# Edge products of a graph layer split into two column halves of TensorE's array

## The reference

```python
xn  = layernorm(x)
agg = segment_sum(edge_weight[:, None] * xn[src], dst, 12500)       # the edge products
h   = relu(((1 + eps) * xn + agg) @ W1.T + b1)
gnn = h @ W2.T + b2
mix = mixer(xn)       # 1x1 product to 768 channels, batch norm, relu, a grouped product, gated linear
                      # attention within groups of 32 channels, a product back to 256 channels, norms
x   = x + gnn + mix
x   = x + ffn(layernorm(x))    # 256 -> 1024 -> 256 with gelu, kept for the top half of the nodes by a routing weight
```

## Time and profile before

| | us |
|---|---|
| median of two runs | 2584.67 |
| the two runs | 2580.34 and 2589.0 |
| span of the profiled execution | 2600.5 |

### The profile page before, as it was taken

One profiled execution on the slowest core, in us unless ns is written; L12 is line 12 of the kernel. 1 busy time (PEld: TensorE's weight loads), 2 busy tenths in 40 slices (PEclk: granted clock), 3 DMA queues, 4 the chain that ended last, 5 costly groups with the idle time before them and its releaser, 6 DMA issues.

```text
span 2600.5 us, 42005 instructions
## 1 busy us (share of the span) xinstructions
PE 2467.0 (95%) x12655; PEld 2165.7 (83%) x12655; DVE 1799.8 (69%) x5988; ACT 1441.2 (55%) x3219; POOL 1793.2 (69%) x1881
## 2 busy tenths in 40 slices
PE   4789999999999999999999999999999999999996
PEld 4777888878888887888888888888788888888886
DVE  8847775776766767667677676676866767767657
ACT  3545665645656656556565565565655656556531
POOL 1247777777777777777777777777777777777600
PEclk9889999999999999999999999999999999999998
DMA  6734444344344343443444434434344344343338
GB/s 205 254 109 117 117 117 124 113 119 124 113 120 121 115 129 113 120 123 114 124 119 118 124 113 120 123 114 129 113 120 124 113 124 119 113 128 113 111 117 282
DMA packets 192004, 333.43 MB, mean 128 GB/s; under 512 B 46286, under 2 KB 133964, under 8 KB 191672
## 3 DMA queue, kind: packets, MB, share of 16 engines
q0 software_dynamic: 86752, 238.17, 31.9%
q1 hardware_dynamic: 105018, 92.42, 11.2%
HBM read 291.99 MB, written 38.46 MB: 127 GB/s over the span
## 4 chain that ended last, share of the span: by engine, by line
PE 79%; DVE 9%; DMA 6%; ACT 4%; issue 1%; POOL 1%; SPq 0%; DVEq 0%
PE bank L1169 24%; PE qkv L1264 13%; PE bank L1276 12%; PE bank L1183 9%; PE bank L1213 6%; PE qkv L1193 4%; DMA work<-in_x 4%; PE qkv L1192 2%; PE bank L1229 2%; PE bank L1238 2%; PE bank L1203 2%; DVE rings L972 1%; DMA xn_dram<-work 1%; DMA rings<-xn_dram,window 1%; POOL rings L778 1%
## 5 line engine op out<-in xcount | busy, mean ns | idle before, releaser
L778 POOL DMA_INDIRECT rings<-xn_dram,window x1764 | 1767.5, 1002 | 592.0 <-issue 381.7
L1169 PE MATMUL bank<-rings 128*128 128x256 f32 x3528 | 891.6, 381 | 28.8 <-DVE rings L972 15.1
L1169 PEld LDWEIGHTS bank<-rings 128*128 128x128 f32 x3528 | 654.9, 190 | 130.0 <-DVE rings L972 30.6
L972 DVE TENSOR_SCALAR rings<-iota,window_dst,window 128x128 f32<-128x128 f32 x1764 | 556.3, 359 | 143.6 <-PE bank L1169 128.6
L1264 PE MATMUL qkv<-work,ffn_weights 128*128 128x256 f32 x1568 | 362.9, 380 | 0.0
L1276 PE MATMUL bank<-ffn_weights,work 128*128 128x256 f32 x1568 | 362.0, 379 | 0.0
L868 ACT ACTIVATE work<-qkv,fb 128x256 f32<-128x256 f32 x392 | 160.0, 473 | 310.1 <-PE qkv L1264 309.6
L1276 PEld LDWEIGHTS bank<-ffn_weights,work 128*128 128x128 f32 x1568 | 297.2, 190 | 40.0
L1264 PEld LDWEIGHTS qkv<-work,ffn_weights 128*128 128x128 f32 x1568 | 293.9, 190 | 37.8
L1183 PE MATMUL bank<-resident,weights 128*128 128x256 f32 x1176 | 280.6, 382 | 0.0
L1183 PEld LDWEIGHTS bank<-resident,weights 128*128 128x128 f32 x1176 | 225.5, 192 | 31.2
(11 more groups left out here) (241 smaller groups left out, 3288.0 us busy)
## 6 DMA issues: line engine op xcount, KB each, us to landing
rings<-xn_dram,window POOLq DMA_INDIRECT x1764, 2.8
xn_dram<-work SPq DMA_DIRECT2D x14, 896.0 KB, 8.4
work<-xn_dram SPq DMA_DIRECT2D x49, 256.0 KB
work<-in_x SPq DMA_DIRECT2D x48, 256.0 KB
out<-work SPq DMA_DIRECT2D x48, 256.0 KB
work<-in_x SPq DMA_DIRECT2D x7, 896.0 KB, 7.8
rings<-in_x SPq DMA_DIRECT2D x6, 896.0 KB, 9.5
rings<-out SPq DMA_DIRECT2D x6, 896.0 KB, 8.5
```

Of the source, the lines that this page charges most:

```text
L778: nc.gpsimd.indirect_dma_start(out=msg[q][:, :], out_offset=None, in_=xn_dram[:, :], in_offset=bass.IndirectOffsetOnAxis(ap=window[t % WIN ...
L972: v.tensor_scalar(sel[k % SEL_RING], iota[:, :], window_dst[b][:, k % SLOTS:k % SLOTS + 1], window[b][:, k % SLOTS, 2:3].bitcast(F32), ALU ...
L1169: te.matmul(agg[h][:, 0:D], sel[k % SEL_RING], msg[q], start=first, stop=last, skip_group_check=True).then_inc(slot_used, 1)
```

## The change

Each edge product becomes two. The first takes columns 0 to 63 of `sel` as its stationary operand and writes partitions 0 to 63 of `agg[h]`; the second takes columns 64 to 127 and writes partitions 64 to 127. Both stream the whole `msg[q]` of 128 x 256. The built program gives the first the array's columns 0 to 63 (tile size 128 x 64, position 0, 0) and the second columns 64 to 127 (position 0, 64); every other matmul of the main part keeps 128 x 128. The semaphore is raised by the second product alone.

```diff
                 pe.wait_ge(sel_ready, i * STEP_SLOTS + (k + 1))
                 pe.wait_ge(msg_landed[q], i * (16 * TURNS) + 16 * (k // RING + 1))
-                te.matmul(agg[h][:, 0:D], sel[k % SEL_RING], msg[q], start=first, stop=last,
-                          skip_group_check=True).then_inc(slot_used, 1)
+                for half in range(2):
+                    r = slice(half * P // 2, (half + 1) * P // 2)
+                    ins = te.matmul(agg[h][r, 0:D], sel[k % SEL_RING][:, r], msg[q], start=first, stop=last,
+                                    skip_group_check=True)
+                ins.then_inc(slot_used, 1)
```

## The result

The changed kernel takes 2779.73 us in the median of two runs (2779.47 and 2779.99), against 2584.67 before: a ratio of 1.0761 (95% interval 1.0739 to 1.0782), 195 us slower. The forecast was 2870 us. The direction held. Of the terms of the sum, those for the order of the passes and for alternating halves were far too large and the one for the borders far too small, and the errors nearly made up for each other.

A forecast was written before the change was run, and what follows sets the result against it. The prediction took PE to bound the kernel; 151 + 85 + 63 - 14 = +285 us on the profiled span of 2600.5 gave 2886, or 2870 us on the median of 2584.67, with an 8 in 10 range of 2700 to 3400.

The forecast's parts named there:

- the order of the passes: At each group's end, the second half runs one pass late: 0.216 us for each of 701 groups, 151 us.
- alternating halves: When PE goes between halves, a matmul starts 0.03 us later for its weights: 85 us (0 to 170).
- the borders: Changes between full and half width, 1402 of them, cost 0.09 us per group: 63 us (0 to 313).
- PE bounds, and the halves run beside each other: In the edge products, what PE does longer the kernel does longer; both column halves run at once, 0.432 us per product.
- serial rival: The two halves of an edge product never run at once: 0.864 us per edge, 3381 us in all; chance 0.22.
- rival of the paired passes: PE runs both halves' first passes together within a group: +70 us, 2655 us in all; chance 0.06.
- the added bounds: Sum of all terms' bounds: +122 to +447 us, 2707 to 3032 us, with 126 us at most for changes of width.
- the nearest row: A late weight load in the old trace, taken as the cost per width change: 0.03 us half, 0.06 full.
- the rival of the emptying: PE empties at each change between full and half width: 313 us in place of 63, 3120 us in all; chance 0.25.
- Waiting: Of PE's own 28.8 us of waiting before edge products, a slower PE loses some: -14 us (0 to -29).

## Why the prediction was right, and where it was wrong

*PE bounds, and the halves run beside each other.* Right: 0.432 us per slot within a group, and the runs with one half alone (no gain) and with both in the same half (688 us more) show it from both sides. The serial rival, 3381 us, is out.

*The order of the passes costs a half edge per group, 151 us.* Wrong, the step that failed. It took the passes to start in the order of the program, so that the second half runs one pass late. They start in pairs, 6 to 7 ns apart, and the run with the halves apart shows that another product between the two halves in the kernel doesn't hinder it: the pairs are 13 to 14 ns apart there. The term measured nothing. The rival of the paired passes had this right, at a chance of 0.06; its ground against it, that matmuls start in program order in the trace, rested on a trace in which all products but the two records of line 310 want all columns, so that it could not have shown another order.

*Alternating halves, 85 us.* Wrong with it: there is no alternation to pay for. The second passes' two weight loads start at 1402.35 and 1402.36, 0.21 us ahead of their matmuls, and one slot more costs 0.43 us. What is left is the distance of 6 to 7 ns between the two starts, once per group: 5 us.

*Borders, 63 us within 0 to 313.* Too small by a factor of nearly four: 230 us without the halves' distance, and above the 126 that the upper end of the added bounds took. The loads come late as the nearest row had it, but cost 0.105 and 0.051 us where 0.06 and 0.03 were taken, and PE stops for 0.093 us besides, in both directions. That is the rival of the emptying in kind, at less than its price: 0.163 us to the end of the record was taken, and the next load starts 0.07 us before that modelled end. The run with a half and two quarters shows that a change of width stops PE even between columns that are free: the quarters begin 0.31 us behind the half's second pass, where 0.216 is the stream's own distance. In these runs the change takes 0.093 us of stop and 0.02 to 0.105 of late load.

*Waiting, -14 us within 0 to -29.* Too small: 235 - 178 = 57 us don't show in the span. The lists of waits show 31 of them, at lines 1171 and 1195; the rest is not told apart further, and part of it will lie at borders where PE had stopped already. Against the medians 40 don't show, since the profiled run of the kernel before lasted 15.8 us longer than its median.

So the sum of the measured terms, 0 + 5 + 230 - 57 = 178 us of span, stands against the forecast's 151 + 85 + 63 - 14 = 285. The direction and the bound were reasoned; that the time came within 90 us of the forecast was luck, since 231 us too much for order and alternation stood against 167 too little for the borders. Two rivals, the paired passes and, at a lower price, the emptying at each border, came true together; each was priced alone, and none of the cases joined them.

## What to carry to other kernels

Column halves of one fp32 product run side by side here, but a product that fills the array anyway gained nothing from being cut: a slot takes 0.43 us whole, in halves and in quarters, since every pass streams the same moving data for just as long. What it can lose is at the borders: in these traces TensorE stops where the width of the stationary tile changes, and the weights of the next product aren't loaded ahead, some 0.15 us on the way in and 0.15 to 0.20 on the way out with 256 columns of moving data, whatever the number of products between. So count changes of width in the engine's order, not products; if narrow tiles are needed, keep them together, or give their neighbours the same width, which left 30 us here of a loss of 195.
